# The per-partition maximum of a masked tile: two reductions of 1024 columns replaced by one of 2048, at another place in VectorE's order

## The reference

```python
# per batch b, with the weights of its session
h   = gelu(xm.T @ W_sess[ids[b]] + b_sess[ids[b]])       # 128 channels -> 256 hidden
o   = (h @ W2 + b2) * (time < lens[b])                   # 256 -> 128 rows, masked in time
# then one 2048 x 2048 layer over the last axis, in fp8, with scales over whole tensors
w_scale = 448 / max(max|weight|, EPS);    w_q = fp8_e4m3(weight * w_scale)
o_scale = 57344 / max(max|o|, EPS);       o_q = fp8_e5m2(o * o_scale)
out = x + (o_q @ w_q.T) / o_scale / w_scale + bias
```

## Time and profile before

| | |
|---|---|
| median of 3 runs | 842.91 us (841.18 to 843.74) |
| the profiled execution | 841.9 us, span 840.1 us |
| TensorE busy | 831.3 us (99%) |
| VectorE busy | 479.9 us (57%) |
| ScalarE / GpSimd busy | 321.4 (38%) / 440.7 us (52%) |
| L626, the scans of o | 64, 77.6 us together |

### The profile page before, as it was taken

The page is one execution under the profiler, slowest core; times in us unless marked ns, Lnnn a source line. Parts: engine busy times, 40 slices in busy tenths (PEclk is TensorE's granted clock), DMA queues, the critical chain, the costliest instruction groups (busy, mean ns, idle before and its releaser), DMA issues.

```text
span 840.1 us, 10029 instructions
## 1 busy us (share of the span) xinstructions
PE 831.3 (99%) x3518; PEld 470.7 (56%) x3518; DVE 479.9 (57%) x497; ACT 321.4 (38%) x338; POOL 440.7 (52%) x193
## 2 busy tenths in 40 slices
PE   8999999999999999999999999999999999999998
PEld 5666766676766767675444444444444444444444
DVE  7979998788888888888432323232323232332322
ACT  7777777888988898883000000000000000000000
POOL 2633434799999999995643232424242424242421
DMA  8899996677868876665488676767777676768682
GB/s 307 331 354 413 366 342 260 232 292 287 308 250 310 347 276 248 252 250 168 159 271 279 212 275 221 266 230 257 242 245 252 234 266 221 275 215 284 213 262 101
DMA packets 73166, 222.06 MB, mean 264 GB/s; under 512 B 37418, under 2 KB 39474, under 8 KB 52786
## 3 DMA queue, kind: packets, MB, share of 16 engines
q1 hardware_dynamic: 72672, 221.66, 73.6%
q10 hardware_dynamic: 466, 0.04, 0.0%
HBM read 144.35 MB, written 69.21 MB: 254 GB/s over the span
## 4 chain that ended last, share of the span: by engine, by line
PE 93%; DMA 2%; POOL 2%; DVE 1%; issue 1%; ACT 0%; SPq 0%; DVEq 0%; POOLq 0%
PE ps_h L891 51%; PE ps_h L810 20%; PE ps_o L831 12%; PE ps_o L825 10%; DMA wqT<-in_L_ffn_weight 2%; POOL ws L446 1%; DMA o_in<-in_L_cond_W_sess 1%; POOL wqT L448 1%; DVE o_and_max L621 0%; POOL xl L439 0%; DVE wc L639 0%; DVE wE L637 0%; PE ps_o L891 0%; PE ps_h L867 0%; PE ps_o L810 0%
## 5 line engine op out<-in xcount | busy, mean ns | idle before, releaser
L891 PE MATMUL ps_h<-wqT,x_sb 128*128 128x512 bf16 (+1 forms) x2048 | 441.4, 378 | 1.3 <-POOL wqT L448 1.0
L891 PEld LDWEIGHTS ps_h<-wqT,x_sb 128*128 128x128 fp8e5 x2048 | 200.0, 98 | 241.3 <-issue 2.4
L439 POOL TENSOR_TENSOR xl<-x_sb,xh 128x1024 fp32r<-128x1024 f32 x62 | 149.6, 2413 | 86.1 <-ACT xh L481 86.0
L810 PE MATMUL ps_h<-xh,whl 128*128 128x512 f32 x508 | 157.0, 430 | 1.9 <-DVE hl L611 1.4
L463 POOL TENSOR_TENSOR x_sb<-x_sb,bias_sb 128x2048 f32<-128x2048 f32 x16 | 72.3, 4520 | 143.7 <-DMA x_sb<-in_x 143.7
L463 POOL TENSOR_TENSOR h<-h,bias_sb 128x2048 f32<-128x2048 f32 x16 | 72.2, 4514 | 130.8 <-DMA h<-in_x 130.8
L730 DVE SCALAR_TENSOR_TENSOR o_and_max<-ps_h,scales,h 128x512 f32<-128x512 f32 x64 | 47.7, 746 | 154.4 <-PE ps_h L891 149.4
L730 DVE SCALAR_TENSOR_TENSOR o_and_max<-ps_h,scales,x_sb 128x512 f32<-128x512 f32 x64 | 47.7, 749 | 144.4 <-PE ps_h L891 139.3
L810 PEld LDWEIGHTS ps_h<-xh,whl 128*128 128x128 f32 x508 | 94.9, 188 | 50.2 <-issue 28.6
L831 PE MATMUL ps_o<-h,w_sb 128*128 128x512 f32 x256 | 120.3, 592 | 0.0
L621 DVE SCALAR_TENSOR_TENSOR o_and_max<-ps_o,b_sb,steps 128x1024 f32<-128x1024 f32 (+1 forms) x65 | 82.2, 1265 | 31.4 <-PE ps_o L831 31.0
(11 more groups left out here) (82 smaller groups left out, 456.5 us busy)
## 6 DMA issues: line engine op xcount, KB each, us to landing
x_sb<-in_x SPq DMA_DIRECT2D x47, 1024.0 KB, 5.2
masked_out<-o_and_max SPq DMA_DIRECT2D x32, 1024.0 KB, 5.2
o_in<-masked_out SPq DMA_DIRECT2D x32, 1024.0 KB, 9.0
out<-o_and_max SPq DMA_DIRECT2D x31, 1024.0 KB, 5.1
h<-in_x SPq DMA_DIRECT2D x16, 1024.0 KB, 7.2
wt<-in_L_ffn_weight SPq DMA_DIRECT2D x42, 384.0 KB, 5.3
wqT<-in_L_ffn_weight SPq DMA_DIRECT2D x19, 832.0 KB, 9.0
wraw<-split_w SPq DMA_DIRECT2D x28, 256.0 KB, 4.9
```

Of the source, the lines that this page charges most:

```text
L439: pool.tensor_tensor(xl[:, u % 2, :], x_cols(u), xh[:, u % 2, :].bitcast(fp32), ALU.subtract)\
L810: mm = nc.tensor.matmul(to[:, cols], whl[:, b % DIRECT, rows], xs[:, u % 2, cols], start=(k == 0), stop=(k == 2))
L891: mm = nc.tensor.matmul(bank, qT[:, r, k // 2, :, k % 2], wq[:, n, k, cols], start=(k == 0), stop=(k == KT - 1))
```

## The change

`scan_o` of a whole unit is no longer called in each turn. In each even turn `u` from 2 to 62 a new function `scan_batch(u / 2 - 1)` reduces both units of the batch that is complete, 2048 columns, with one instruction, and it stands behind `split_h_rest(u + 1)` and ahead of the weight's scan. In turn 63 unit 62 is scanned alone, and unit 63 in halves as before; the three results of the last batch go to two columns and to the last reduction. `o_max` shrinks from 65 to 34 columns. So 62 reductions of 1024 columns become 31 of 2048.

```diff
-        o_max = sb("o_max", [P, UNITS + 1], fp32)
+        o_max = sb("o_max", [P, B + 2], fp32)
...
+            def scan_batch(b):
+
+                dve.wait_ge(o_masked, (b + 1) * UPB)
+                dve.tensor_reduce(o_max[:, b:b + 1], o_sb[:, b % 2, :], AX.X, ALU.max, apply_absolute_value=True)\
+                   .then_inc(o_scanned, 1)
+
             def scan_o(u, k, cols):
                 dve.wait_ge(o_masked, u + k + 1)
-                dve.tensor_reduce(o_max[:, u + k:u + k + 1], o_cols(u)[:, cols], AX.X, ALU.max, apply_absolute_value=True)\
+                dve.tensor_reduce(o_max[:, u - B + 1:u - B + 2], o_cols(u)[:, cols], AX.X, ALU.max, apply_absolute_value=True)\
                    .then_inc(o_scanned, 1)
...
                     mask_o(u - 1, start, 0, slice(0, UNIT))
-                    scan_o(u - 1, 0, slice(0, UNIT))
                 if 0 <= u - QUANT - 1 < EARLY_CHUNKS:
                     round_at(u - QUANT - 1)
...
                 if u + 1 < UNITS:
                     split_h_rest(u + 1)
+                if u >= UPB and u % UPB == 0:
+                    scan_batch(u // UPB - 1)
+                if u == UNITS - 1:
+
+                    scan_o(u - 1, 0, slice(0, UNIT))
                 if 1 <= u <= SCANS:
                     scan(u - 1)
...
-            dve.wait_ge(o_scanned, UNITS)
+            dve.wait_ge(o_scanned, B + 1)
...
-            dve.wait_ge(o_scanned, UNITS + 1)
+            dve.wait_ge(o_scanned, B + 2)
```

More of the change, by code:

```diff
@@ L433, in _ @@
             pool.memset(w_max[:, SCANS:SCANS + 1], EPS).then_inc(floor_ready, 1)
-            pool.memset(o_max[:, UNITS:UNITS + 1], EPS).then_inc(floor_ready, 1)
+            pool.memset(o_max[:, B + 1:B + 2], EPS).then_inc(floor_ready, 1)
             pool.memset(ones[:, :], 1.0).then_inc(ones_ready, 1)
```

## The result

Measured against the kernel before in 22 runs of each, the changed kernel has a median of 843.94 us (842.65 to 846.19) and the one before 841.94 us (840.05 to 844.88). The ratio is 1.0022, with a 95% interval of 1.0015 to 1.0029: slower by 1.9 us (1.3 to 2.4), clear of zero and just under the 0.3% that the prediction called the same. The prediction had + 2.15. Its 845.1 lies 1.2 above the median, of which 0.97 is that its base, the median of three runs, was that much above the one of 22 runs.

A forecast was written before the change was run, and what follows sets the result against it. TensorE bounds the kernel, busy for 831 of 840 us, so VectorE matters only where TensorE waits. Terms - 0.61 + 1.06 + 1.70 = + 2.15 us on the median 842.91 give 845.1, range 842.2 to about 848.2.

The forecast's parts named there:

- Price of the reduction: On VectorE, one reduction of 2048 columns lasts 2.28 us, 2.19 from start to start; one batch saves 0.07 us.
- The end: In turn 62 the long reduction delays the mask of unit 62 and the last reduction: loss 1.70 us.
- The weight's maximum: In turns 20 and 21 the maximum of the weight's maxima, which TensorE waits for, comes later: loss 1.06 us.
- The early turns: In turns 5 to 9, where scans wait for a DMA, `split_h_rest` starts earlier: gain 0.61 us.
- Steady turns with the weight's scan: In turns 1 to 20, `split_h_rest` starts at P + 0.07 in odd turns, 0.20 us to spare: cost 0.
- P: The start of `project1` on TensorE, from which its turns are measured; a turn without loss takes 5.89 us.
- the limit: The latest start of `split_h_rest` that costs TensorE nothing, P + 0.27.
- Turns with rounding: In turns 23 to 61, `split_h_rest` starts earlier than the P + 0.06 of before: cost 0.
- The clock: Rival: between the stages TensorE's longer wait lowers its clock to 1.2 GHz: + 3.3 us, 848.4; chance 0.07.
- the scan turns: Rival: an unhidden register load costs nine pairs 0.08 us each and the end 0.28: + 3.1, 846.0; chance 0.10.
- late landings: Rival: more late weight pieces in odd turns, each gaining up to 1.14 us; with six, 838.8 us; chance 0.05.
- The rival of the covered end: Between the stages transfers set the step, not the last reduction; 1.70 goes, + 0.45 stays: 843.4 us; chance 0.08.

The follow-up runs named there:

- both: The changed kernel with batch 30 reduced ahead of the last `split_h_rest` and batch 9 behind the weight's maximum; ratio 0.9993 to the kernel before.
- end_early: The changed kernel with the reduction of batch 30 ahead of the last `split_h_rest` instead of behind it; ratio 1.0003 to the kernel before.
- max_first: The changed kernel with batch 9 reduced in turn 21 behind the weight's maximum, not in turn 20 ahead of it; ratio 1.0018 to the kernel before.
- early_only: The kernel before with the change in turns 1 to 20 alone, batch 9 reduced in turn 21 behind the weight's maximum; ratio 0.9989 to the kernel before.
- extra512: The changed kernel with one more reduction of 512 columns, result unused, behind each batch's reduction in turns 2 to 18; ratio 1.0053 to the kernel before.
- two_reductions: The changed kernel with each batch reduced by two instructions of 1024 columns in the same place; ratio 1.0028 to the kernel before.
- old_place: The changed kernel with each batch's reduction behind the mask of even turns, ahead of the rounding and `split_h_rest`; ratio 1.0234 to the kernel before.

## Why the prediction was right

- **Price of the reduction.** 2.28 us predicted, 2.275 measured; 2.19 from start to start, as predicted.
- **The end.** + 1.70 predicted; + 1.71 between the traces. Taking it back gave 1.6 us in time, putting it alone into the kernel before cost 1.4. The register load was hidden, as I had taken it.
- **The weight's maximum.** + 1.06 predicted; + 0.81 between the traces. This term was too large by 0.25. The mask of turn 21 is followed after 1.20 us, not 1.31; and VectorE's 0.15 us of idle time ahead of this mask, which the prediction had left out, went into the long piece. TensorE had no margin, as the prediction had it: the maximum comes 0.82 later behind the turn's start (4.53 to 5.35 us) and TensorE's matmul 0.81. In time, both against end_early gives 0.8; max_first alone gives 0.3, within its interval of either.
- **The early turns.** - 0.61 predicted, - 1.62 between the two traces. That trace pair flatters the change: landings differed. The medians, with the two terms above, leave 1.85 - 1.71 - 0.81 = - 0.67 for all the rest, and early_only has - 0.9 with an interval of - 1.9 to + 0.1. So the sign is likely and the size is open between about 0 and 1.9; that the sum came out 0.3 from the measured + 1.85 while this term is open is in part luck.
- **Steady turns with the weight's scan: no loss.** Right. `split_h_rest` starts earlier than forecast (P - 0.02 in place of P + 0.07, by the 0.11 us that the mask no longer costs), and extra512 shows the limit behind it.
- **Turns with rounding: no loss.** Right but for the 0.3 us above, and for a gain of 0.14 in turn 53 that the prediction had not seen. What makes them free is the place: in the old place the same instruction costs 16 us and more.
- **Rivals.** The clock didn't fall: in 390 to 394 us TensorE is busy for 2.29 us of 4 and the granted clock is 1.00, 2.4 GHz, as in the earlier trace rows.

```profile
390.00:394.00 4.00, 2.29 (x12) 1.08 (x13) 3.15 (x10) 0.69 (x2) 0.00 (x0) 1.00 0.97 393
```

  The end wasn't covered, the scan turns did recover, and late landings did not outweigh the rest. The rival of the covered end had a grain of truth: with the reduction out of the way (end_early, both), and in one of three traces of the kernel before, the transfers are the bound, by 0.3 us.
- **Two slips in the working.** Against the rival of the scan turns it cites that the mask at 108.23 follows without a gap. That mask is of an odd unit (15), for which no register is loaded, so the row says nothing of the load. The conclusion holds all the same: the masks of the even units 2 to 18 start 0.08 to 0.09 us before the end of the weight's scan too. And the bounds and the spread as stated give 842.91 + 0.25 - 1.7 = 841.5 to 842.91 + 3.7 + 0.8 = 847.4, not 842.2 to 848.2; the measured 843.94 lies in both.

No version tried is clear of the kernel before. The best are the changed order without its two losses (both, 0.9993) and the early turns alone (0.9989), each with 1 or more at the upper end of its interval.

## What to carry to other kernels

Merging two operations on an engine that isn't the bound saves little (0.07 us here); the length of one piece and what stands behind it decide. Look for the few turns that differ from the steady ones: the last one, and one with a one-off result that the bounding engine waits for. A long piece that is free in 29 of its 31 places cost 1.7 and 0.8 us in the two others. Fill an engine's known wait with the long piece, and don't let it follow the wait.

## What the runs showed of the hardware that was not expected

- A VectorE operation that waits for the semaphore of the operation directly ahead of it starts 0.11 us later than one that doesn't (1.31 against 1.20 us behind a mask of 1024 columns). The two short operations of the rounding show it too: the second, which waits for the first, starts 0.03 to 0.04 us behind its end, while `split_h_rest` behind them starts 0.08 us before the end of the second.
- A store of 1 MB took 7.7 to 9.5 us until the next transfer could go out when a load of 1 MB had been issued 1.0 us ahead of it (seven traces), 4.5 to 5.1 us when that load was 2.7 us ahead (five), and 4.9 us when the load came 0.4 us behind it (one). An earlier store thus finished later in absolute terms than a later one: 399.04 in end_early against 395.24 in the changed kernel.
- The turns 23 to 62 sum to 233.6 to 233.8 us in seven traces (old order, but also extra512 and two_reductions) and to 234.1 in the other five, all of the new order (old_place, with its long turns, is left out); no cause was found. The trace of the kernel before has both kinds in itself: 5.89 or 5.90 us in turns 11 to 20, 5.87 or 5.88 in turns 24 to 52.
